# Half as many gram products, in alternating halves of PSUM, and the first norms on three engines

## The reference

```python
x_norm = _rmsnorm(x, norm_weight)
k = _phi(jnp.einsum('btd,fd->btf', x_norm, Wk))     # 64 key features
v = jnp.einsum('btd,ed->bte', x_norm, Wv)           # 128 value features
def step(M, kv):
    k_t, v_t = kv
    v_pred = jnp.einsum('bf,bfd->bd', k_t, M)
    surprise = jnp.linalg.norm(v_t - v_pred, axis=-1, keepdims=True)
    M = M + eta_c[None, :, None] * surprise[:, :, None] * (k_t[:, :, None] * v_t[:, None, :])
    return (_ln2(M), None)
M, _ = jax.lax.scan(step, M0, (kT, vT))
q = _phi(jnp.einsum('btd,fd->btf', x_norm, Wq))
output = x + jnp.einsum('btd,ed->bte', jnp.einsum('btf,bfd->btd', q, M), Wout)
```

## Time and profile before

| | |
|---|---|
| Median of 3 executions | 274.84 us (274.27 to 275.19) |
| Profiled execution: span from its first to its last instruction | 273.0 us; no other time of that execution is given |
| PE busy | 258.6 us, 95% |
| DVE, ACT, POOL busy | 215.7 us (79%), 192.7 us (71%), 100.9 us (37%) |
| Granted TensorE clock, mean | 0.993 of full speed |

### The profile page before, as it was taken

How to read it: one execution, slowest core, us unless ns; L and a number is a source line. 1 busy time by engine, 2 the same in 40 slices (tenths; PEclk the granted TensorE clock), 3 DMA queues, 4 the chain that set the end, 5 groups by cost and what they waited for, 6 DMA issues and landing times.

```text
span 273.0 us, 5442 instructions
## 1 busy us (share of the span) xinstructions
PE 258.6 (95%) x1792; PEld 169.9 (62%) x1796; DVE 215.7 (79%) x733; ACT 192.7 (71%) x469; POOL 100.9 (37%) x130
## 2 busy tenths in 40 slices
PE   7899999999977889999999999999999999999993
PEld 2379945466663644967877776778786444444482
DVE  6977579999999589899899988777950798666684
ACT  1497479886656479788776789998861898777730
POOL 9314000000000067898875589599775000000000
PEclk9999999999999799999999999999999999999999
DMA  7700000000000190400000000000000000000005
GB/s 199 214 15 2 2 0 4 0 1 0 2 2 0 25 413 29 154 2 4 0 2 0 2 0 1 4 0 0 2 0 2 0 1 0 4 0 0 0 18 141
DMA packets 8303, 8.51 MB, mean 31 GB/s; under 512 B 1745, under 2 KB 7378, under 8 KB 7762
## 3 DMA queue, kind: packets, MB, share of 16 engines
q1 hardware_dynamic: 7442, 7.65, 8.7%
q10 hardware_dynamic: 832, 0.49, 0.6%
HBM read 7.09 MB, written 1.05 MB: 30 GB/s over the span
## 4 chain that ended last, share of the span: by engine, by line
PE 58%; DVE 30%; issue 4%; ACT 3%; DMA 2%; POOL 1%; SPq 0%; DVEq 0%; ACTq 0%; POOLq 0%
PE PS L867 10%; PE PS L866 10%; PE PS L839 7%; PE PS L816 7%; PE PS L829 4%; DVE arena L1608 3%; PE PS L501 3%; PE PS L520 3%; DVE arena L1840 2%; DVE arena L1839 2%; DVE arena L1595 2%; DVE mxb L1854 2%; DVE arena L1627 2%; DVE arena L1636 2%; DMA x<-L_attn_x 2%
## 5 line engine op out<-in xcount | busy, mean ns | idle before, releaser
L866 PE MATMUL PS<-arena 128*128 128x512 f16 x128 | 48.5, 379 | 0.0
L867 PE MATMUL PS<-arena 128*128 128x512 f16 x128 | 48.5, 379 | 0.0
L1912 DVE TENSOR_TENSOR arena<-arena 128x512 f32<-128x512 f32 x32 | 22.1, 692 | 13.0 <-ACT arena L1304 13.0
L816 PE MATMUL PS<-arena 128*128 128x512 f32 (+3 forms) x80 | 31.9, 530 | 0.3 <-ACT arena L1273 0.3
L1303 ACT ACTIVATE arena<-PS,arena 128x512 f32<-128x512 f32 x32 | 22.9, 716 | 9.1 <-PE PS L867 9.1
L1368 POOL CAST arena<-arena 128x512 f16<-128x512 f32 x2 | 1.3, 644 | 72.8 <-ACT x L1166 72.8
L1360 POOL TENSOR_TENSOR arena<-arena 128x256 f32<-128x256 f32 x32 | 21.6, 674 | 15.8 <-DVE arena L1846 13.0
L1273 ACT ACTIVATE arena<-PS,lnt 128x512 f32<-128x512 f32 (+3 forms) x40 | 24.8, 628 | 3.2 <-DVE lnt L1861 3.1
L1361 POOL TENSOR_TENSOR arena<-arena,small 128x256 f16<-128x256 f32 (+1 forms) x36 | 23.8, 661 | 2.8
L1304 ACT ACTIVATE arena<-PS,arena 128x512 f16<-128x512 f32 x32 | 22.8, 714 | 0.0
L1854 DVE TENSOR_REDUCE mxb<-PS 128x1 f32<-128x512 f32 (+3 forms) x40 | 22.1, 600 | 0.0
(11 more groups left out here) (282 smaller groups left out, 641.8 us busy)
## 6 DMA issues: line engine op xcount, KB each, us to landing
arena<-h_T SPq DMA_DIRECT2D x2, 1024.0 KB, 5.8
x<-L_attn_x SPq DMA_DIRECT2D x4, 256.0 KB, 4.5
arena<-cos SPq DMA_DIRECT2D x1, 1024.0 KB, 4.8
arena<-sin SPq DMA_DIRECT2D x1, 1024.0 KB, 7.1
arena<-w_T SPq DMA_DIRECT2D x3, 256.0 KB, 3.1
out<-arena SPq DMA_DIRECT2D x2, 256.0 KB, 2.3
con<-shape_constants ACTq DMA_DIRECT2D x1, 192.0 KB, 3.3
out<-arena SPq DMA_DIRECT2D x1, 192.0 KB, 2.1
```

The lines of the kernel that those rows point to most:

```text
L816: i = mm(PS[:, k, 0:cnt * P], qT1[:, t * P:(t + 1) * P], kT1[:, c * P:(c + cnt) * P], start=True, stop=not last)
L866: mm(bank(b), wH[:, k, m * P:(m + 1) * P], sH[:, k, cols], start=(k == 0), stop=False)
L867: i = mm(bank(b), wL[:, k, m * P:(m + 1) * P], sL[:, k, cols], start=False, stop=(k == HT4 - 1))
L1912: v.tensor_tensor(RP[m], FP[m], high, ALU.subtract).then_inc(rest_ready, 1)
```

## The change

It has four parts.

- **Values, two lanes a product.** The stationary operand of a value product is now 64 columns of `VT` (four groups of 16 tokens), and the moving one the 17 columns of lane s and the 17 of lane s+2. Lanes s and s+1 go to partitions 0 to 63 and 64 to 127. 64 products make what 128 made.
- **Keys, without the neighbour's copies.** `KU` now holds 528 tokens in a row for the keys and as many for the scaled keys. A product takes 32 tokens of both at once, token by token (`KP`, a stationary operand whose neighbouring columns lie 528 elements apart). The copies of L1485 and L998 are gone. It is still one product per two lanes, 64 in all, but they too alternate between the halves of the partitions.
- **Copies.** The results lie otherwise in PSUM, so the copies to `G` have other shapes, run over the lanes innermost, and are split otherwise between ACT and DVE. The copies to `CC` are two per bank where they were one (keys and scaled keys now stand token by token in `G`).
- **First norms on three engines.** Of the `XR` norms ACT takes tiles 5, 6, 7 and 15. All 16 `xn` norms move from DVE to POOL. DVE turns chunks 2 and 3 to `xrT` (`turned`), ACT copies value chunk 3.

Six norms stand ahead of the first `VX` copies, five ahead of the last ones. The core of the diff:

```diff
-        KU = take(SH * 2 * L).rearrange("p (c t i) -> p c t i", c=SH, t=2)
+        KW = T // 4 + HALF
+        KU = take(2 * 2 * KW).rearrange("p (g i t) -> p g t i", g=2, t=2)
+        KP = KU.rearrange("p g t i -> p g i t")
...
+        ACT_NORMED = (5, 6, 7, 15)
+        DVE_NORMED = [n for n in range(NT) if n not in ACT_NORMED]
...
-            def values_gram(r):
-                b, s0, cnt = V_RUNS[r]
-                for s in range(s0, s0 + cnt):
-                    i = mm(PS[0:L, b, (s - s0) * (HALF + 1):(s - s0 + 1) * (HALF + 1)], VT[:, HALF * s:HALF * s + L], VX[:, s, :], start=True, stop=True)
+            def value_product(b, at_, s):
+                o = s % 2
+                return mm(PS[64 * o:64 * o + 64, b, at_:at_ + 2 * HG], VT[:, HALF * s:HALF * s + 64], VX[:, s:s + 3:2, :], start=True, stop=True)
+            def key_product(b, at_, o, c):
+                t0 = HALF * (c % K2)
+                return mm(PS[64 * o:64 * o + 64, b, at_:at_ + 2 * HG], KP[:, c // K2, t0:t0 + L, :].rearrange("p i t -> p (i t)"),
+                          UX[:, c, :, :].rearrange("p h j -> p (h j)"), start=True, stop=True)
...
-                f(CC[:, 0:3, r0:r0 + cnt, :], PS[0:W, b, 0:cnt * 3 * L].rearrange("p (j q t) -> p q j t", q=3, t=L), ACT.Copy).then_inc(lanes_act, 1)
+                have = PS[0:W, b, 0:cnt * 3 * L].rearrange("p (j c) -> p j c", c=3 * L)
+                f(CC[:, 0:2, r0:r0 + cnt, :], have[:, :, 0:2 * L].rearrange("p j (t q) -> p q j t", q=2), ACT.Copy).then_inc(lanes_act, 1)
+                f(CC[:, 2, r0:r0 + cnt, :], have[:, :, 2 * L:3 * L], ACT.Copy).then_inc(lanes_act, 1)
...
+            def normed(first, end):
+                for n in range(first, end):
+                    if n % 8 == 0:
+                        pool.wait_ge(rstd_ready, n // 8 + 1)
+                    nc.gpsimd.tensor_scalar(xn[:, n, :], x[:, n, :], mv[:, n, 0:1], lnt[:, 0, n:n + 1], ALU.subtract, ALU.mult).then_inc(xn_ready, 1)
...
+            normed(0, 6)
+            values(0)
+            values(1)
+            normed(6, 11)
+            values(2)
+            values(3)
+            normed(11, NT)
...
-            for n in range(NT):
-                v.tensor_scalar(xn[:, n, :], x[:, n, :], mv[:, n, 0:1], lnt[:, 0, n:n + 1], ALU.subtract, ALU.mult).then_inc(xn_ready, 1)
```

More of the change, by code:

```diff
@@ new lines, in values_gram, with keys_gram @@
+            def values_gram(g):
+                values_in(pe, 2 * g + 1)
+                pe.wait_ge(vx_ready, 2 * g + 2)
+                for k in range(PAIRS):
+                    for o in range(2):
+                        i = value_product(V_BANK[g], k * 2 * HG, value_lanes_from(g, k) + o)
+                i.then_inc(vgram_done, 1)
+            def keys_gram(part):
+                b, g, k0, k1 = KEY_PARTS[part]
+                pe.wait_ge(ux_ready, 2 * g + 2)
+                pe.wait_ge(ku_act, 1 if g == 0 else 2)
+                for k in range(k0, k1):
+                    for o in range(2):
+                        i = key_product(b, (k - k0) * 2 * HG, o, K2 * g + PAIRS * o + k)
+                i.then_inc(gram_done, 1)
@@ new lines, in rest_gram @@
+            def rest_gram():
+                pe.wait_ge(k_ready, 2)
+                for g in range(2):
+                    for o in range(2):
+                        value_product(REST_BANK, g * 2 * HG, value_lanes_from(g, PAIRS) + o)
+                pe.wait_ge(ux_ready, 4)
+                pe.wait_ge(ku_act, 5)
+                for g in range(2):
+                    for o in range(2):
+                        i = key_product(REST_BANK, (4 + 2 * g) * HG, o, K2 * g + 2 * PAIRS + o)
+                i.then_inc(vgram_done, 1)
@@ L960, in deviations_in, with rms_normed @@
                 f(lnt[:, 0:2, 8 * h:8 * h + 8], lnt[:, 0:2, 8 * h:8 * h + 8], ACT.Sqrt).then_inc(sd_ready, 1)
+            def rms_normed(h):
+                act.wait_ge(rstd_ready, h + 1)
+                for n in range(8 * h, 8 * h + 8):
+                    if n in ACT_NORMED:
+                        f(XR[:, n, :], x[:, n, :], ACT.Identity, scale=lnt[:, 1, n:n + 1], bias=lnt[:, 6, n:n + 1]).then_inc(xr_act, 1)
             def values_out(ch):
@@ L1005, in next_keys, with keys_gram @@
-                f(KU[h0, K2 * (g + 1) - 1, 1, HALF:L], KU[h1, c, 0, 0:HALF], ACT.Copy, scale=etac[h1, 0:1]).then_inc(ku_act, 1)
-            def keys_gram(r):
-                act.wait_ge(gram_done, r + 1)
-                for h in range(2):
-                    i = f(*gram_lanes(r, h), ACT.Copy)
-                i.then_inc(gram_act, 1)
+                f(KU[h0, g, :, BANK:KW], KU[h1, g + h, :, 0:HALF], ACT.Copy).then_inc(ku_act, 1)
+            def keys_gram(part):
+                act.wait_ge(gram_done, part + 1)
+                f(*keys_lanes(part, 0), ACT.Copy).then_inc(gram_act, 1)
@@ L1013, in _ @@
+            deviations_in(0)
+            rms_normed(0)
+            act.wait_ge(early_in, 16 * 4)
+            for b in range(2):
+                act.wait_ge(xrt_done, b + 1)
+                f(xrT[:, b * BANK:(b + 1) * BANK], bank(b), ACT.Copy, scale=normw[:, 0:1]).then_inc(xrt_act, 1)
+            deviations_in(1)
+            f(small[:, 39:40], normw[:, 0:1], ACT.Exp)
+            rms_normed(1)
+            act.wait_ge(set_once, SET)
+            values_out(0)
+            values_out(1)
             keys(0)
-            act.wait_ge(xrt_done, 3)
@@ L1505, in _ @@
+            for e in range(2):
+                values_gram(1, e)
+            for e in range(2):
+                rest_gram(*rest_values_lanes(1, e))
+            rest_gram(*rest_keys_lanes(1))
+            keys_gram(1)
+            keys_gram(2)
             aT, bT, V = (CC[:, q, 1:HALF + 1, :] for q in range(3))
```

219 lines of the change are left out of this document (107 added, 112 removed).

## The result

| | before | after |
|---|---|---|
| Median of 4 executions | 274.88 us (274.27 to 275.19) | 266.43 us (266.00 to 266.60) |
| Ratio | | 0.9685, 95% interval 0.9654 to 0.9715 |
| Profiled execution | span 273.0 | 266.38 us, span 264.6 |
| Granted TensorE clock, mean | 0.993 | 1.0 |

The account below looks back on a forecast made before the run. PE's grams, limited by weight loads, were taken to bound the head; the turn of `G` 6.5 us earlier, less 0.2 for `CC` copies, gave -6.3: span 266.7, median 268.5 us; own range 267.0 to 269.5, 8 in 10 266.8 to 271.8.

Parts of the forecast that it names:

- Grams, 256 records at 30 ns, 7.7 us: PE's value and key products: pairs in alternating column halves overlap, 7.7 us instead of 16.4.
- First gram at 16.2: PE's first gram starts 2.5 us later, behind the second square root, table load, tile 15's norm and copies.
- the sharing with POOL: Four of DVE's first five norms each wait for a POOL norm: 0.42 us instead of 0.26, +0.65 us.
- Copies end with PE: Copies to `G` end with PE or just behind; the turn of `G` starts 0.8 us behind the last gram.
- copies bind: Rival: strided PSUM reads and strided writes add up, the turn of `G` waits for ACT, 269.5 to 270.5 us; chance 0.13.
- Copies to `CC`, +0.2: Two copies per bank delay DVE's first table by 0.2 us, bounds 0.1 and 0.8.
- `xn` norms leave DVE "at no gain": Moving 16 norms (4.2 us) off DVE gains nothing, since DVE waited for PE; POOL pays 7 us, ending near 25.
- Everything from there on shifted by one constant: Behind DVE's first table the order is unchanged, so the head's saving arrives at the end in full.
- From the span to the median, +1.84: The median lies 1.84 us above the profiled span: span 266.7 gives 268.5 us.
- No overlap: Rival: short products' weight loads go one behind the other, 58 ns per record, 275.6 us, slower; chance 0.07.
- POOL starts late: Rival: fetching POOL's code takes some 6 us and delays `VX` copies and grams by 2.2, 270.7 us; chance 0.05.
- Less than that in the way: Rival: the lock costs nothing, copies at 0.8 ns, first gram 15.5, 266.8 us or a little below; 0.06 below 267.

Follow-up runs that it names:

- e1: Changed kernel with all gram products of one PSUM half ahead of those of the other, so neighbours don't alternate between halves: 271.71 us.
- e6: Changed kernel with all 16 of POOL's `xn` norms placed behind the four `VX` copies: 271.53 us.
- e12: e8 with POOL's `xn` norms placed later, 0, 5 and 11 instead of 6, 5 and 5 around the `VX` copies: 266.94 us.
- e8: Changed kernel with DVE instead of ACT making the two copies of the odd lanes of the first value part: 265.94 us.
- e10: Kernel before with only its 16 `xn` norms moved from DVE to POOL: 273.92 us.
- e7: Changed kernel with the 16 `xn` norms back on DVE in one block, ahead of its copies of key part 0: 272.84 us.
- e11: Changed kernel with 16 more one-column memsets on DVE, in its wait at 17.9 us: 267.20 us.
- e2: Changed kernel with 60 unread products behind the grams, 30 with stationary columns 8 elements apart, then 30 with contiguous ones: 271.25 us (one run).

## Why the prediction was right, and where it was wrong

Against the steps of the prediction:

- **Grams, 256 records at 30 ns, 7.7 us.** Measured 1.75 + 1.80 + 1.98 + 2.19 = 7.72, from the starts of the groups. e1 shows that the alternation does it. The evidence, two long key products in the two halves in the earlier trace rows, held for products of 34 columns. By the Trainium skill ("TensorE: Matmul & The Clock Gate", section "The mechanism") a weight load overlaps with products in flight only when the row group differs; here the row groups are the same and the column halves differ, and the trace doesn't agree: records start 29 ns apart, and 58 apart inside one half (e1).
- **First gram at 16.2.** 15.82. The term that was too large is the sharing with POOL, +0.65 at the second square root (11.85, forecast 12.2): DVE's first five norms took 1.36 us, 0.27 each instead of 0.42. e6 and e12, without POOL's norms there, bring the first gram 0.2 us earlier: that is the term's real size. Its premise was wrong too: I made the term from POOL's duration, estimated at 0.42 and measured at 0.79, and from DVE's waiting a whole one each time.
- **Keys and values 3.0, last `VX` copy +0.2.** 2.93 and no wait. PE's last gram ended at 26.47, forecast 27.1.
- **Copies end with PE.** Nearly: 255 elements took 0.63 us as in the earlier trace rows, but a 510-element copy with neighbouring destinations took 0.59. ACT had 12 copies, not 13, and took 4.5 us from 22.64 on, as forecast. The turn started 0.94 behind the last gram (forecast 0.8). The rival "copies bind" held for 0.2 to 0.3 us (e8).
- **Copies to `CC`, +0.2.** +0.06 (27.41 to 28.71 is 1.30; before, 34.39 to 35.63 was 1.24).
- **Head: -6.3.** -6.93.
- **`xn` norms leave DVE "at no gain".** Right for the head, as a term of a sum that starts from before (in e10 the gain lies behind the head), wrong as a statement on the change: with the shorter grams their cover on PE was gone, and left on DVE in one block they cost 6.4 us (e7). Their cost on POOL was 13.5 us, not 7; that they still ended at 26.2 (forecast near 25) is due to the idle time that POOL had between the `VX` copies. The edge is not far, as e6 and e12 show.
- **"Everything from there on shifted by one constant".** This is the step that failed and put the time outside the range: whatever lay behind the head stood at nothing, for no other reason than that its order is unchanged. Behind the head the shift grew from 6.93 to 8.41, in these steps: 0.5 at the loop's check from the clock, 0.37 and 0.19 from the place of DVE's instructions (e11), 0.30 in the attention, which goes with the instructions on POOL (e7, e10), 0.27 ahead of the 27th scan, and -0.12 at one step of the loop. The last two divide the three programs built from before from the eleven built from after, and their cause stays open. The clock's 0.5 lies between the two executions profiled and is not shown to come from the change. Such a term could have been put into the range beforehand: the granted clock of the earlier trace rows's execution was at half from 88.50 to 91.91 us. I had even used that stage as evidence: the loads of 330 ns of L669 in the earlier trace rows, which I took for the price of row halves, lie in it. The same line of after, at the full clock, has 182 to 188.
- **From the span to the median, +1.84.** Luck. The span of 273.0 and the median of 274.84 belong to different executions. Within one execution before's time is 2.08 to 2.25 us above its span and after's 1.78 to 1.90; with before's own difference the forecast would have been some 0.3 us higher.
- **The rivals.** No overlap: did not happen. POOL starts late: no stall behind the pool's setup (8.1, first norm at 8.72). "Less than that in the way", with 0.06, named the time (266.8 or a little below) but not the reason: the first gram came at 15.82 and not 15.5, and the larger part of what was missing lay behind the head.

The prediction had the likeliest mechanism and its size to 0.02 us, and missed the range because it left out what lay behind the head: 1.48 us, of which 0.86 go with the place and the number of DVE's and POOL's instructions, 0.5 with the clock of the execution, and 0.1 to 0.2 stay open.

## What to carry to other kernels

Short products whose time is weight loads run at nearly twice the rate when neighbours write to different column halves; look for long products that already do it in the trace. When an engine's work gets shorter, price again every edit that was free because it lay beside it: here 16 norms whose place made no difference in the old kernel's head cost 6.4 us in the new one, and each late operation came back through another engine's queue, so follow the queue as well as the wait. And put 0.5 to 1 us of a range aside for what moves behind the stage that changes (granted clock, place of instructions), and compare the clock at one place over several kernels before calling it a work of the change.

## What the hardware did that I had not expected

- Weight loads of 64 columns 8 elements apart: 60 ns a record where neighbouring columns take 31, both in alternating halves (e2).
- A 128x128 norm on GpSimd with two per-partition factors: 0.79 us alone, 1.00 to 1.03 beside DVE's copies and tables (e6, e12). VectorE needs 0.26 to 0.30 for the same.
- Sharing between the two came in two sizes. Norms, tables and products of two operands lost 0.1 to 0.2 us each beside GpSimd's norms: 0.2 us in the head for six of these, 1.29 us in e12. The attention's casts on DVE, 0.29 us alone, waited whole: over the fourteen traces all 129 that began more than 0.15 us ahead of the end of a GpSimd instruction ended 0.15 or 0.16 us behind that end. A GpSimd product in after, and the cast that began inside it:

```profile
170.96 1.26 POOL L1465 TENSOR_TENSOR arena<-arena 128x512 f32<-128x512 f32 x1
...
171.20 1.17 DVE L1930 CAST arena<-arena 128x256 f16<-128x256 f32 x1
```

  In e10 a DVE copy of 0.60 us took 1.49 in the same way, and a GpSimd norm beside it 1.35. By the Trainium skill ("SBUF — State Buffer", section "SBUF: two separate sides") the shared pair is an exclusive lock for a whole instruction, which DVE takes with two inputs in SBUF or in a mode of two ports. The trace agrees for these casts and that copy, and not for the products of two operands: 14 took 2.66 us instead of 2.22 in e12, where one GpSimd norm is 0.79.
- DVE lost 0.19 us at one scan and 0.37 at a branch when 16 instructions stood ahead of them that could as well stand elsewhere, and GpSimd 0.34 at one product when it had 16 instructions fewer. In before 8 KB of instructions are fetched at 77.89, 0.9 us behind the first hole, and in e11 at 70.87, 0.7 behind the same one; after has no fetch between 69 and 72.3. By the Trainium skill ("Runtime: NRT & Kernel Launch", section "Instruction fetch mechanics") instructions stream in blocks, and crossing one is mostly hidden. That the holes are such crossings fits the times; no run here shows it.
